# Later inverse deviations on GpSimd, first-norm transposes behind the next scores, and a new table of filler matmuls

## The chip, the cores and the metric

The kernel runs on one core of one Trainium2 chip. Its time is device microseconds for one execution. It was run three times: median 441.17 us, lowest 440.37, highest 441.78. One more execution was profiled; all rows below come from that one. Five engines work at once, each on its own queue of instructions, and meet through semaphores: TensorE (PE, with PEld for its weight loads), VectorE (DVE), ScalarE (ACT), GpSimd (POOL) and SyncE (SP, which only issues DMAs here).

## What is computed

A masked convolution with a row-by-row gated recurrence comes first (its scan runs over 16 rows). Its result, 16 images of 256 tokens with 96 channels, then goes through one transformer layer:

```python
x = _L0_conv_ref(x, w_i2s, w_s2s, w_skip, b_skip)
t = _to_tokens(x)
t = t + _L1_attn_ref(_ln_t(t), Wq, Wk, Wv, Wp, bp)      # causal, 6 heads of 16
t = t + _L1_ffn_ref(_ln_t(t), gate_w, gate_b, w1, b1, w2, b2)
x = _from_tokens(t, x)
...
def _ln_t(v, eps=1e-05):
    m = jnp.mean(v, axis=-1, keepdims=True)
    s = jnp.var(v, axis=-1, keepdims=True)
    return (v - m) / jnp.sqrt(s + eps)
...
# _L1_ffn_ref: 4 experts, the best 2 of a token kept and renormed
h = jax.nn.gelu(jnp.einsum('bsd,edh->ebsh', x, w1) + b1[:, None, None, :], approximate=False)
y = jnp.einsum('ebsh,ehd->ebsd', h, w2) + b2[:, None, None, :]
out = jnp.einsum('bse,ebsd->bsd', masked, y)
```

## The kernel before

The convolution and its recurrence take about the first 75 us. What follows is eight **passes** over blocks of two images: 512 tokens, as four **tiles** (s = 0 to 3) of 128 tokens. In the code a pass is `body(n, ...)`, once for each engine. Pass 0 is `first`, pass 7 is `last`, passes 1 to 6 are alike and follow one another at a fixed distance.

Attention inside a pass is cut into ten **units** u = 0 to 9 (`UNITS`): one tile's queries with three heads (tiles 0 and 2) or two heads (tiles 1 and 3). Units 0 and 1 are tile 0, units 2 to 4 tile 1, units 5 and 6 tile 2, units 7 to 9 tile 3. A unit goes through all engines:

- `scores(u)` on PE, into one of two PSUM banks;
- `row_max(u)` on DVE, `exps(u)` on ACT, `recip(u)` on DVE (one over the row sums);
- `scale(u)` on POOL, which multiplies the probabilities by those reciprocals;
- `probs_t(u)`, called T(u) here, on PE: transposes of the probabilities. It waits for `scale(u)`;
- `take_pt(u)`: a copy out of PSUM, on ACT for the units in `PT_ON_ACT`, on DVE for 0, 3, 5 and 7;
- `values(u)` on PE, and at a tile's end `heads_out(s)` (ACT), `project_out(s)` (PE) and `attn_residual(s)` (DVE), which adds the residual and takes mean and variance for the second norm.

The second norm then needs `rstd2(s)` on POOL (two small instructions, a sum and a power -0.5, called the pair here) and `normalize2(s)` on DVE. The expert layer of the pass stands at its end: transposes of the normed tokens, twelve hidden chunks, and routing.

The second expert matmul of pass n-1 is kept as **filler** for PE in pass n: 48 parts `expert_out(n-1, parts)`, 12 for each tile, each two matmul instructions; the first part of a tile has a bias matmul in front (the `b2hl` one). `FILL[j]` says how many parts stand in **slot** j, the piece of the pass's code with T(j) in it; what `FILL` leaves (12 parts, tile 3) is done behind the last slot. When a tile's 12 parts are done, DVE's `combine(s)` weighs its four experts' results: four instructions, put by line 831 into the slot after the one that holds the tile's last part. The first norm of pass n+1 runs in pass n's slots as well: `tokens_first` in slot 1, `norm1` and `rstd1` in slot 2, `normalize1` in slot 3, `channels_first` (four transposes of the normed tokens on PE) in slot 4, and `x1_rest` on DVE in slot 5.

Nothing is scheduled by a tool. Each engine's order is the order of the calls in its `body`, and an engine that waits holds up all that stands behind it in its own queue. The places that matter for the steps below:

- PE, lines 1090 to 1109: in slot j first `scores(j+2)`, then the filler, then `values`, then T(j), then `channels_first` (slot 4) and `project_out`.
- DVE, lines 821 to 843: in slot j `row_max(j+2)`, `recip(j+1)`, `take_pt(j)`, `x1_rest` (slot 5), `combine`, the norm steps, then `attn_residual` and `normalize2`.
- POOL, lines 452 to 459: in slot j `scale(j+1)`, then `rstd1` (slot 2), then `rstd2`.

Of the kernel before, what the change touches and what calls it, by code (L numbers as in the profile page):

```python
# [23 lines left out]
ALU = mybir.AluOpType  # L24
# [14 lines left out]
SPB = 4  # L39
# [12 lines left out]
NU = len(UNITS)  # L52
TILE_END = [1 + max(u for u, (a, t, _) in enumerate(UNITS) if 2 * a + t == s) for s in range(SPB)]

FILL = [16, 3, 3, 2, 3, 3, 2, 2, 2, 0]
TAIL = SPB * NCH - sum(FILL)
TAIL_EARLY = min(TAIL, 9)
PT_ON_ACT = (1, 2, 4, 6, 8, 9)
# [6 lines left out]
def hybrid_kernel(nc, x, w_input, w_state, b_skip, wq, wk, wv, wp, bp,  # L65
                  gate_w, gate_b, w1, b1, w2, b2, ident, ident_bf, causal_bf, lower, out):
    with ExitStack() as ctx:
# [331 lines left out]
        def _(pool):  # L399
# [9 lines left out]
            def rstd1(n):  # L409

                wait_alone(pool, ln1_aggr, 4 * n + 4)
                nc.gpsimd.tensor_scalar(ve1[:], mv1[:, :, 1], 1e-5, None, ALU.add).then_inc(rs1_step, 1)
                pool.wait_ge(rs1_step, 2 * n + 1)
                nc.gpsimd.tensor_tensor(rs1[:], ve1[:], nhalf[:], ALU.pow).then_inc(rs1_step, 1)

            def rstd2(n, s):
                wait_alone(pool, ln2_aggr, 4 * n + s + 1)
                nc.gpsimd.tensor_scalar(ve2[:, s:s + 1], mv2[:, s, 1:2], 1e-5, None, ALU.add).then_inc(rs2_step, 1)
                pool.wait_ge(rs2_step, 8 * n + 2 * s + 1)
                nc.gpsimd.tensor_tensor(rs2[:, s:s + 1], ve2[:, s:s + 1], nhalf[:, 0:1], ALU.pow).then_inc(rs2_step, 1)  # L420

# [28 lines left out]
            def body(n, first=False, last=False):  # L450
                scale(n, 0)
                for j in range(NU):
                    if j + 1 < NU:
                        scale(n, j + 1)
                    if j == EARLY_T0 + 1 and not last:
                        rstd1(n + 1)
                    for s in range(SPB - 1):
                        if j == TILE_END[s] + 1:
                            rstd2(n, s)
                rstd2(n, SPB - 1)  # L460
                keep_t1(n, first)
                if not last:
                    residual(n + 1)
                    x1_whole(n + 1)
# [157 lines left out]
        def _(dve):  # L622
# [131 lines left out]
            def normalize2(n, s):  # L754
                dve.wait_ge(rs2_step, 8 * n + 2 * s + 2)
                V.tensor_scalar(xh2[:, s], t1[:, s], mv2[:, s, 0:1], rs2[:, s:s + 1],
                                ALU.subtract, ALU.mult).then_inc(xh2_done, 1)
# [55 lines left out]
            def body(n, first=False, second=False, last=False):  # L813
# [7 lines left out]
                for j in range(NU):  # L821
# [17 lines left out]
                    for s in range(SPB - 1):  # L839
                        if j == TILE_END[s] + 1:  # L840
                            attn_residual(n, s, first)
                        if j == TILE_END[s] + 2:
                            normalize2(n, s)
                attn_residual(n, SPB - 1)
                if not last:
                    q_rest(n + 1)
# [32 lines left out]
        def _(pe):  # L879
# [207 lines left out]
            def body(n, first=False, last=False):  # L1087
                tail = [divmod(i, NCH) for i in range(SPB * NCH - TAIL, SPB * NCH)]
                for j in range(NU):
                    if j:  # L1090
                        if j + 2 < NU:
                            scores(n, j + 2)
                        if not first:
                            expert_out(n - 1, out_parts(j))
                        for u in VALUES_AT.get(j, ()):
                            values(n, u, first)
                    else:
                        start = [] if first else out_parts(0)
                        expert_out(n - 1, start[:NCH])
                        scores(n, 2)  # L1100
                        expert_out(n - 1, start[NCH:])
                    probs_t(n, j, first)
                    if j == EARLY_T0 and not last:
                        pe.wait_ge(v_done, n + 1)
                        tokens_first(n + 1)
                    if j == EARLY_XT and not last:
                        pe.wait_ge(t1_done, 4 * n + 1)
                        channels_first(n + 1)
                    for s in range(SPB - 1):
                        if j == TILE_END[s] + 1:  # L1110

# [145 lines left out]
```

## Time and profile before

| | |
|---|---|
| median of three runs | 441.17 us (440.37 to 441.78) |
| profiled execution | 441.85 us, of which the span from first to last instruction is 439.9 us |
| PE busy | 412.5 us, 94% of the span |
| DVE, ACT, POOL busy | 264.9, 252.1, 147.7 us |
| one pass of passes 1 to 6 | 42.17 us |
| granted TensorE clock | 0.987 on the mean; 1.00 in passes 1 to 7 |

A timeline row gives the start of a group in us from the span's start, the time from its first start to its last end, engine, line, operation, output and inputs, and a count. Ends of matmuls are modelled and overlap the next one, so the pace of PE is read from one start to the next. In brackets stands the idle time of the engine just before, and what ended it.

### The profile page before, as it was taken

The numbers are of one execution on the slowest core, as the hardware profiler recorded it, in microseconds if no ns is written. First come the engines' busy times: TensorE is split into PE (matmuls) and PEld (weight loads), VectorE is DVE, ScalarE is ACT, GpSimd is POOL, SyncE is SP. The second block draws the span as 40 slices with busy tenths as digits, with TensorE's granted clock in tenths as the row PEclk, the third lists the DMA queues.
The fourth block names the chain that finished last, engine by engine and source line by source line (L and its number), as shares of the span: only waits on it lengthen the run. The fifth ranks groups of instructions, "written<-read, shape, count | busy, mean of one in ns | idle before, by whom it ended". The sixth has DMA issues, their size and how long they took to land.

```text
span 439.9 us, 10654 instructions
## 1 busy us (share of the span) xinstructions
PE 412.5 (94%) x3226; PEld 346.7 (79%) x3226; DVE 264.9 (60%) x888; ACT 252.1 (57%) x701; POOL 147.7 (34%) x313
## 2 busy tenths in 40 slices
PE   4999999788899999999999999999999999999896
PEld 4999996455578878877887788788877887788686
DVE  2799998457416861785287538744863586267415
ACT  2333333356487648765865596568656764876380
POOL 6000000625513632462156305531543254236200
PEclk9999999969999999999999999999999999999999
DMA  8600000210021012101210120022002100210000
GB/s 185 168 0 0 0 0 19 63 30 17 9 60 44 3 34 53 39 1 42 52 31 0 48 55 22 0 55 52 18 0 61 46 0 7 77 24 4 7 14 18
DMA packets 16472, 14.94 MB, mean 34 GB/s; under 512 B 7586, under 2 KB 13588, under 8 KB 16452
## 3 DMA queue, kind: packets, MB, share of 16 engines
q1 hardware_dynamic: 14788, 13.87, 12.5%
q10 hardware_dynamic: 1472, 0.68, 0.6%
q8 instruction: 10, 0.16, 0.2%
q0 software_dynamic: 192, 0.15, 0.1%
q14 instruction: 10, 0.08, 0.1%
HBM read 3.86 MB, written 1.57 MB: 12 GB/s over the span
## 4 chain that ended last, share of the span: by engine, by line
PE 62%; DVE 16%; issue 10%; POOL 5%; ACT 2%; DVEq 1%; DMA 1%; ACTq 1%; POOLq 0%; SPq 0%
PE F L1057 13%; PE T L1015 6%; PE A L1036 6%; PE F L1073 4%; PE F L1077 4%; PE F L1074 4%; PE S L999 3%; POOL p_sb L435 3%; PE S L1001 3%; DVE fc L660 2%; DVE ig L659 2%; PE S L1004 2%; DVE t_cm L678 2%; DVE xh L713 1%; DVE nmax L735 1%
## 5 line engine op out<-in xcount | busy, mean ns | idle before, releaser
L435 POOL TENSOR_SCALAR p_sb<-p_sb,rden 128x128 f32<-128x128 f32 (+1 forms) x192 | 79.7, 431 | 121.1 <-DVE rden L741 119.0
L1057 PE MATMUL F<-w_sb,hid 128*128 128x96 f32 x768 | 97.6, 272 | 0.0
L1057 PEld LDWEIGHTS F<-w_sb,hid 128*128 128x128 f32 x768 | 95.6, 192 | 0.0
L551 ACT ACTIVATE p_sb<-S,nmax 128x128 f32<-128x128 f32 (+1 forms) x192 | 78.8, 424 | 12.7 <-DVE nmax L735 12.6
L735 DVE TENSOR_REDUCE nmax<-S 128x2 f32<-128x512 f32 (+1 forms) x80 | 50.5, 632 | 56.8 <-PE S L1004 56.7
L597 ACT ACTIVATE hid<-F,b_sb 128x512 f32<-128x512 f32 x72 | 49.5, 687 | 10.5 <-PE F L1077 9.7
L1015 PE MATMUL T<-id_sb,p_sb 128*128 128x128 f32 x288 | 48.5, 287 | 7.4 <-POOL p_sb L435 6.7
L484 ACT COPY pt_sb<-T 128x512 f32<-128x512 f32 (+1 forms) x48 | 26.4, 550 | 46.0 <-PE T L1015 46.0
L1015 PEld LDWEIGHTS T<-id_sb,p_sb 128*128 128x128 f32 x288 | 31.5, 145 | 17.6 <-POOL p_sb L435 12.2
L999 PE MATMUL S<-k_bd,q_st 96*128 96x384 f32 (+2 forms) x96 | 39.4, 417 | 3.5 <-DMA k_bd<-k_cur 2.7
L551 ACT ACTIVATION_READ_ACCUMULATOR p_sb<-S,nmax 128x1 f32 x192 | 39.7, 207 | 0.0
L1036 PE MATMUL A<-pt_sb,v_cur 128*32 128x128 f32 x576 | 33.9, 281 | 0.7 <-ACT pt_sb L484 0.7
L896 PE MATMUL F<-x_pad,win_sb 96*112 (+1 forms) x192 | 27.2, 291 | 6.2 <-DMA x_pad<-in_x 6.2
L1001 PE MATMUL S<-k_bd,q_st 96*128 96x384 f32 (+2 forms) x96 | 32.7, 348 | 0.0
L810 DVE SCALAR_TENSOR_TENSOR y_sb<-F,gw,y_sb 128x96 f32<-128x96 f32 x96 | 30.5, 317 | 3.4
L506 ACT ACTIVATE tc_sb<-cell 48x128 f32<-48x128 f32 x32 | 9.8, 307 | 37.7 <-DVE cell L662 37.7
L1073 PE MATMUL F<-x2hi,w1hi 96*128 96x512 f32 x72 | 29.9, 416 | 1.4 <-ACT x2hi L592 0.8
L896 PEld LDWEIGHTS F<-x_pad,win_sb 96*112 96x112 f32 x192 | 24.9, 193 | 6.1 <-DVE win_sb L632 6.1
L1077 PE MATMUL F<-x2lo,w1hi 96*128 96x512 f32 x72 | 29.2, 406 | 0.0
L1074 PE MATMUL F<-x2hi,w1lo 96*128 96x512 f32 x72 | 28.5, 395 | 0.0
L1036 PEld LDWEIGHTS A<-pt_sb,v_cur 128*32 128x32 f32 x576 | 21.5, 110 | 8.7 <-ACT pt_sb L484 5.5
L484 DVE COPY pt_sb<-T 128x384 f32<-128x384 f32 (+1 forms) x32 | 20.0, 624 | 13.0 <-PE T L1015 13.0
(142 smaller groups left out, 789.6 us busy)
## 6 DMA issues: line engine op xcount, KB each, us to landing
k_bd<-k_cur SPq DMA_DIRECT2D x93, 32.0 KB, 2.0
q_st<-q_cur SPq DMA_DIRECT2D x28, 96.0 KB, 2.2
k_bd<-k_cur SPq DMA_DIRECT2D x93, 16.0 KB, 1.8
t_st<-t_cm SPq DMA_DIRECT2D x7, 192.0 KB, 2.4
out_y<-y_sb SPq DMA_DIRECT2D x7, 192.0 KB, 1.9
x_pad<-in_x SPq DMA_DIRECT2D x2, 612.0 KB, 7.1
w_sb<-in_w SPq DMA_DIRECT2D x1, 576.0 KB
hid<-in_w SPq DMA_DIRECT2D x1, 576.0 KB, 6.9
```

What stands on the lines that cost most here:

```text
L435: last = nc.gpsimd.tensor_scalar(p, p, rden[:, u % 3, i:i + 1], 1.0, ALU.mult, ALU.mult)
L484: copy(pt_sb[:, u % NPT, 0:w], T[:, 0:w]).then_inc(pt_done, 1)
L551: last = nc.scalar.activation(p_sb[:, u % 3, i * nk:(i + 1) * nk], S[u % 2][:, i * nk:(i + 1) * nk], ACT.Exp, bias=nmax[:, u % 3, i:i + 1] ...
L597: nc.scalar.activation(hid[:, c, :], L1[c % 4][:], ACT.Gelu, bias=b1_sb[:, c:c + 1]).then_inc(gelu_done, 1)
L735: V.tensor_reduce(nmax[:, u % 3, 0:HG[t]], S[u % 2][:, 0:HG[t] * nk].rearrange("p (h k) -> p h k", k=nk), AX.X, ALU.max, negate=True).then ...
L896: last = mm(G[q][0:GATE_M, c * HC:(c + 1) * HC], wi_sb[:, tap, c], xr[:, bs, tap:tap + W], start=(c == 0 and tap == 0), stop=ready, skip_g ...
L999: mm(d, q_st[:, g, ts], k_bd[:, a, 0, g, i0:i1, 0:nk], start=(3 * g + i0 == h0), stop=False, skip_group_check=True)
L1015: last = nc.tensor.transpose(T[:, i * TT:(i + 1) * TT], p_sb[:, u % 3, i * TT:(i + 1) * TT], id_sb[:])
L1036: last = mm(A[VW * (h % 3):VW * (h % 3) + VW, 0:TT], v, pt_sb[:, u % NPT, c0:c0 + TT], start=(kt == 0 and h < 3), stop=(kt == t and h >= 3 ...
L1057: last = mm(dst[:, e * C:(e + 1) * C], hid[:, c, s * TT:(s + 1) * TT], w2_sb[:, c], start=False, stop=(c == NCH - 1), skip_group_check=True)
L1073: mm(dst, w1hi[:, cs], x2hi[:], start=True, stop=False)
L1077: mm(dst, w1hi[:, cs], x2lo[:], start=False, stop=True).then_inc(hid_ready, 1)
```

## The change

Four things, all in the order of work, and one in a POOL instruction's form:

- `rstd2(s)` on POOL moves one slot later for tiles 0 and 1: the pair of tile 0 stands behind `scale(5)` instead of `scale(4)`, that of tile 1 behind `scale(8)` instead of `scale(7)`. For tile 2 it stays behind `scale(9)`. `normalize2` on DVE moves one slot later with it.
- `channels_first(n+1)` on PE moves from the end of slot 4 to slot 5, behind `scores(7)`.
- `FILL` is new. The running sums of parts were 16, 19, 22, 24, 27, 30, 32, 34, 36, 36; they are 12, 15, 18, 20, 23, 27, 30, 33, 36, 36. The first slot's parts are split 8 and 4 around `scores(2)` instead of 12 and 4.
- From these sums follows more: the bias matmul of tile 1 goes from slot 0 to slot 1, that of tile 2 from slot 4 to slot 5; tile 1's last part (number 23) is in slot 5 instead of slot 3, so `combine(1)` on DVE goes from slot 4 to slot 6.
- The two `tensor_scalar` instructions that add 1e-5 on POOL now multiply by 1.0 and then add.

```diff
-FILL = [16, 3, 3, 2, 3, 3, 2, 2, 2, 0]
+FILL = [12, 3, 3, 2, 3, 4, 3, 3, 3, 0]
+FILL_AHEAD = 8
...
-                nc.gpsimd.tensor_scalar(ve1[:], mv1[:, :, 1], 1e-5, None, ALU.add).then_inc(rs1_step, 1)
+                nc.gpsimd.tensor_scalar(ve1[:], mv1[:, :, 1], 1.0, 1e-5, ALU.mult, ALU.add).then_inc(rs1_step, 1)
...
-                nc.gpsimd.tensor_scalar(ve2[:, s:s + 1], mv2[:, s, 1:2], 1e-5, None, ALU.add).then_inc(rs2_step, 1)
+                nc.gpsimd.tensor_scalar(ve2[:, s:s + 1], mv2[:, s, 1:2], 1.0, 1e-5, ALU.mult, ALU.add).then_inc(rs2_step, 1)
...
-                        if j == TILE_END[s] + 1:
+                        if j == min(TILE_END[s] + 2, NU - 1):
                             rstd2(n, s)
...
-                        if j == TILE_END[s] + 2:
+                        if j == TILE_END[s] + 3:
                             normalize2(n, s)
+                normalize2(n, SPB - 2)
                 attn_residual(n, SPB - 1)
...
                             scores(n, j + 2)
+                        if j == EARLY_XT + 1 and not last:
+                            pe.wait_ge(t1_done, 4 * n + 1)
+                            channels_first(n + 1)
                         if not first:
                             expert_out(n - 1, out_parts(j))
...
-                        expert_out(n - 1, start[:NCH])
+                        expert_out(n - 1, start[:FILL_AHEAD])
                         scores(n, 2)
-                        expert_out(n - 1, start[NCH:])
+                        expert_out(n - 1, start[FILL_AHEAD:])
                     probs_t(n, j, first)
...
-                    if j == EARLY_XT and not last:
-                        pe.wait_ge(t1_done, 4 * n + 1)
-                        channels_first(n + 1)
```

DVE's queue before, in pass 1, slots 4 to 6 (`row_max(6)` to `row_max(8)`, `recip(7)`, `attn_residual(1)`); L810 is `combine(1)`, L756 `normalize2(0)`, L484 `take_pt(5)`, L718 `x1_rest`:

```order
L735 TENSOR_REDUCE nmax<-S 128x3
L741 RECIPROCAL rden<-den 128x3
L810 SCALAR_TENSOR_TENSOR y_sb<-F,gw,t1p 128x96
L810 SCALAR_TENSOR_TENSOR y_sb<-F,gw,y_sb 128x96 x3
L756 TENSOR_SCALAR xh<-t,mv,rs 128x96
L735 TENSOR_REDUCE nmax<-S 128x2
L741 RECIPROCAL rden<-den 128x3
L484 COPY pt_sb<-T 128x384
L718 TENSOR_TENSOR x1lo<-M,x1hi 96x512
L735 TENSOR_REDUCE nmax<-S 128x2
L741 RECIPROCAL rden<-den 128x2
L748 TENSOR_TENSOR t<-M,tb 128x96
```

The same place in the changed kernel (its lines are one higher):

```order
L736 TENSOR_REDUCE nmax<-S 128x3
L742 RECIPROCAL rden<-den 128x3
L736 TENSOR_REDUCE nmax<-S 128x2
L742 RECIPROCAL rden<-den 128x3
L485 COPY pt_sb<-T 128x384
L719 TENSOR_TENSOR x1lo<-M,x1hi 96x512
L757 TENSOR_SCALAR xh<-t,mv,rs 128x96
L736 TENSOR_REDUCE nmax<-S 128x2
L742 RECIPROCAL rden<-den 128x2
L811 SCALAR_TENSOR_TENSOR y_sb<-F,gw,t1p 128x96
L811 SCALAR_TENSOR_TENSOR y_sb<-F,gw,y_sb 128x96 x3
L749 TENSOR_TENSOR t<-M,tb 128x96
```

`combine(1)` stood ahead of `take_pt(5)`; it now stands behind `recip(7)`, ahead of `attn_residual(1)`, `row_max(9)` and `recip(8)`. `normalize2(0)` went from in front of `row_max(7)` to behind `x1_rest`.

POOL's queue before, in pass 0, from `scale(4)` to the pair of tile 2 (L435 is `scale`, three instructions for a unit of three heads and two for one of two heads; L418 and L420 are a pair):

```order
L435 TENSOR_SCALAR p_sb<-p_sb,rden 128x256 x2
L418 TENSOR_SCALAR ve<-mv 128x1
L420 TENSOR_TENSOR rs<-ve,nhalf 128x1
L435 TENSOR_SCALAR p_sb<-p_sb,rden 128x128 x6
L435 TENSOR_SCALAR p_sb<-p_sb,rden 128x256 x2
L418 TENSOR_SCALAR ve<-mv 128x1
L420 TENSOR_TENSOR rs<-ve,nhalf 128x1
L435 TENSOR_SCALAR p_sb<-p_sb,rden 128x256 x4
```

And in the changed kernel:

```order
L436 TENSOR_SCALAR p_sb<-p_sb,rden 128x256 x2
L436 TENSOR_SCALAR p_sb<-p_sb,rden 128x128 x3
L419 TENSOR_SCALAR ve<-mv 128x1
L421 TENSOR_TENSOR rs<-ve,nhalf 128x1
L436 TENSOR_SCALAR p_sb<-p_sb,rden 128x128 x3
L436 TENSOR_SCALAR p_sb<-p_sb,rden 128x256 x4
L419 TENSOR_SCALAR ve<-mv 128x1
L421 TENSOR_TENSOR rs<-ve,nhalf 128x1
L436 TENSOR_SCALAR p_sb<-p_sb,rden 128x256 x2
```

Tile 0's pair went from in front of `scale(5)` to in front of `scale(6)`, tile 1's from in front of `scale(8)` to in front of `scale(9)`.

## Rows read from the trace of the kernel before

**Rows 1.** The page, busy time, share and instructions of each engine.
```profile
PE 412.5 (94%) x3226; PEld 346.7 (79%) x3226; DVE 264.9 (60%) x888; ACT 252.1 (57%) x701; POOL 147.7 (34%) x313
```

**Rows 2.** Stretches: us, busy of PE, PEld, DVE, ACT, POOL, clock, DMA; pass 4.
```profile
259.90:302.07 42.17, 41.15 (x326) 34.14 (x326) 25.35 (x86) 28.07 (x80) 17.12 (x37) 1.00 0.13 33
```

**Rows 3.** Timeline of PE in pass 4.
```profile
263.40 0.42 PE L1053 MATMUL F<-b2hl,ones 128*128 128x384 f32 x1
263.67 1.02 PE L1057 MATMUL F<-w_sb,hid 128*128 128x96 f32 x8
264.53 0.49 PE L1015 MATMUL T<-id_sb,p_sb 128*128 128x128 f32 x3
...
272.38 0.62 PE L1015 MATMUL T<-id_sb,p_sb 128*128 128x128 f32 x4
273.12 0.65 PE L965 MATMUL M<-id_sb,xh 128*96 128x128 f32 x4
273.57 0.49 PE L999 MATMUL S<-k_bd,q_st 96*128 96x512 f32 x1
...
276.02 0.55 PE L1015 MATMUL T<-id_sb,p_sb 128*128 128x128 f32 x3
...
280.40 0.58 PE L1057 MATMUL F<-w_sb,hid 128*128 128x96 f32 x4
281.59 0.66 PE L1015 MATMUL T<-id_sb,p_sb 128*128 128x128 f32 x4 [0.61 <-POOL p_sb L435]
...
283.49 0.66 PE L1015 MATMUL T<-id_sb,p_sb 128*128 128x128 f32 x4
```

**Rows 4.** Timeline of POOL in pass 4.
```profile
262.69 1.08 POOL L435 TENSOR_SCALAR p_sb<-p_sb,rden 128x128 f32<-128x128 f32 x3 [9.91 <-DVE rden L741]
...
271.35 0.94 POOL L435 TENSOR_SCALAR p_sb<-p_sb,rden 128x256 f32<-128x256 f32 x2
...
274.70 1.10 POOL L435 TENSOR_SCALAR p_sb<-p_sb,rden 128x128 f32<-128x128 f32 x3
...
278.60 0.94 POOL L435 TENSOR_SCALAR p_sb<-p_sb,rden 128x256 f32<-128x256 f32 x2 [1.04 <-DVE rden L741]
279.62 0.23 POOL L418 TENSOR_SCALAR ve<-mv 128x1 f32<-128x1 f32 x1
...
280.60 0.94 POOL L435 TENSOR_SCALAR p_sb<-p_sb,rden 128x256 f32<-128x256 f32 x2
281.83 0.94 POOL L435 TENSOR_SCALAR p_sb<-p_sb,rden 128x256 f32<-128x256 f32 x2 [0.29 <-DVE rden L741]
```

**Rows 5.** Timeline of DVE in pass 4.
```profile
274.05 0.29 DVE L810 SCALAR_TENSOR_TENSOR y_sb<-F,gw,t1p 128x96 f32<-128x96 f32 x1
...
275.32 0.33 DVE L756 TENSOR_SCALAR xh<-t,mv,rs 128x96 f32<-128x96 f32 x1
275.56 0.68 DVE L735 TENSOR_REDUCE nmax<-S 128x2 f32<-128x512 f32 x1
...
276.61 0.56 DVE L484 COPY pt_sb<-T 128x384 f32<-128x384 f32 x1 [0.28 <-PE T L1015]
...
278.28 0.15 DVE L741 RECIPROCAL rden<-den 128x2 f32<-128x2 f32 x1
...
279.77 0.16 DVE L741 RECIPROCAL rden<-den 128x2 f32<-128x2 f32 x1
...
282.48 0.26 DVE L748 TENSOR_TENSOR t<-M,tb 128x96 f32<-128x96 f32 x1 [0.82 <-PE M L1042]
...
283.32 0.32 DVE L810 SCALAR_TENSOR_TENSOR y_sb<-F,gw,t1p 128x96 f32<-128x96 f32 x1
```

**Rows 6.** Stretches in pass 0, columns as in Rows 2.
```profile
86.58:89.27 2.69, 0.00 (x0) 0.03 (x1) 2.69 (x3) 2.47 (x2) 1.11 (x2) 1.00 0.52 138
90.00:100.40 10.40, 9.54 (x44) 6.34 (x42) 5.44 (x18) 5.74 (x24) 3.79 (x10) 0.51 0.15 38
...
111.43:112.80 1.37, 0.00 (x1) 0.01 (x1) 1.00 (x3) 0.54 (x3) 1.27 (x4) 1.00 0.02 6
```

## What I expected of the change

> **What bounds the kernel now.** I read four views, in this order. The page's first table says PE is busy 94% of the span and no other engine more than 60% [rows 1], so the first guess is that only PE's own work counts. That share is no proof, since matmul records overlap. The stretch of one pass comes next: passes 1 to 6 each take 42.17 us, at the full granted clock [rows 2], so one pass can be worked through and multiplied. The third view is PE's timeline of such a pass, read from start to start. It shows where PE stands. At T(4), the transposes start at 272.38 and `channels_first` at 273.12, 0.74 later, though four transposes take 0.45 (273.12 to 273.57): about 0.3 is lost to a wait for the normed tokens. At T(8) PE is through its filler by about 280.98 and starts at 281.59, 0.61 later, for POOL's `scale(8)` [rows 3]. These two are what the change is aimed at. The fourth view is the two queues behind T(8). POOL ends `scale(7)` at 279.54, does the pair of tile 1 from 279.62, and only then `scale(8)` at 280.60 [rows 4]. But DVE's `recip(8)` ended at 279.77 + 0.16 = 279.93 [rows 5], so with the pair gone `scale(8)` could start no more than 0.50 sooner: from a reciprocal's end to the scale takes 0.17 (278.28 + 0.15 to 278.60 [rows 4, 5]). **So DVE's queue stands right behind POOL's**, and what the change does to DVE decides. That queue is in order: in slot 8 the last filler is done near 281, so `combine(2)` has its input, DVE then idles 0.82 before 282.48 for a projection, and `combine(2)` still starts at 283.32, after that projection's norm [rows 3, 5].
>
> **The change, part by part.** All shifts are against the same point of pass 4.
>
> *Slot 0, four parts less.* They are 8 matmuls, 263.67 to 264.53, 0.86 us, and the bias of tile 1, 263.40 to 263.67, 0.27 [rows 3]. PE would reach T(0) 1.13 sooner, at 263.40. But T(0) waits for `scale(0)`, which ends at 262.69 + 1.08 = 263.77 [rows 4] and hangs on steps that don't move (exps of unit 0 behind the table load, routing on DVE). T(0) starts at 263.82: 0.71 won, 0.42 turned into a wait. That cover gone, splitting the filler 8 and 4 buys nothing more: `scores(2)` comes sooner, yet T(0) is last. In slot 1 the bias returns (0.27) and I allow 0.1 for PE to fill again behind the stop (0 to 0.2; no row shows it alone). At T(1) 0.33 is left. Slots 1 to 3 hold the same three, three and two parts, so ACT, DVE and POOL all move by the same 0.33.
>
> *Slot 4, the bias of tile 2 gone.* PE comes 0.27 sooner still, but T(4) waits for `scale(4)`, 271.35 + 0.94 = 272.29 [rows 4], less 0.33. T(4) starts at 272.01, 0.37 sooner, and I give its four transposes 0.45 plus 0.05 of the same allowance.
>
> *`channels_first` behind `scores(7)`.* `scores(7)` starts at 272.51, since its bank is free. The wait of 0.3 goes: the tokens are ready long before their new place. `x1_rest` needs them only behind `take_pt(5)`, so the later place costs nothing.
>
> *Slot 5, one part more and the bias.* Before, from `scores(7)` to T(5) was 276.02 - 273.57 = 2.45 [rows 3]. Now 0.45 (`channels_first`), 0.21 (a part is two matmuls of 0.86/8) and 0.27 come in: 3.38. **T(5) starts at 272.51 + 3.38 = 275.89, only 0.13 sooner**, although three parts (0.64) and a wait of 0.3 were taken out ahead of it. The difference is the new waits at T(0) and T(4) and the restarts. It could be as early as `scale(5)` lets it: that is now straight behind `recip(5)`, which ends near 274.1 (the combine next to it starts at 274.05) and moves by 0.3, so 0.17 and 1.10 later it is 275.1 [rows 4, 5]: 0.88 sooner. The other end is 0.2 later.
>
> *`combine(1)` and `normalize2(0)` on DVE.* Behind T(5), `take_pt(5)` starts 0.59 later (276.02 to 276.61 [rows 3, 5]): 276.48. From there to the end of `recip(8)` DVE worked without a stop for 279.93 - 276.61 = 3.32. Into that stretch now come `combine(1)`, 274.05 to 275.32, 1.27, and `normalize2(0)`, 275.32 to 275.56, 0.24 [rows 5]. Both stood earlier, where DVE now has nothing to do: it will idle for over 1 us ahead of `take_pt(5)`, which waits for T(5), with both queued behind. `recip(8)` ends at 276.48 + 3.32 + 1.51 = 281.31, 1.38 later. Behind it on other engines wait `scale(8)` and so T(8); `exps(9)` waits for the `row_max(9)` just ahead.
>
> *The pair of tile 1 behind `scale(8)`.* `scale(8)` starts 0.17 behind `recip(8)`, at 281.48, ends 0.94 later at 282.42, and T(8) starts at 282.47 (0.05 later, as 281.54 to 281.59 before [rows 3, 4]). That is **0.88 later than before**: -0.13 + 1.51 - 0.50. PE has three more parts in slots 6 to 8 to fill the wait, and still stands there for more than 1 us.
>
> *The pair ahead of `scale(9)`.* It starts 0.08 behind `scale(8)` and holds POOL for 0.98 (279.62 to 280.60). `scale(9)` runs from 283.48 to 284.42, T(9) starts at 284.47 instead of 283.49 [rows 3, 4]: 0.98 later. The way through PE from T(8) to T(9) took 1.90, so it would be at 284.37; POOL is last by 0.1.
>
> *Costed at nothing.* `normalize2(1)` now waits on DVE for the pair, with `attn_residual(2)` behind it, some 0.3; PE's last values, q and k projections lie between T(9) and the next projection and cover it, and without that cover it would cost 0.3. The pair of tile 0 ahead of `scale(6)` ends in time for T(6), which has one part more in front. The two-op form: the trace has only one-op adds of 0.23 and two-op scales of 0.36 for 128 columns (1.08 for three) [rows 4]; I take 0, between -0.1 and +0.1, with at most two of five in a pass on the path. No DMA and no queue of SP is touched. Behind T(9) all of a pass hangs together and moves as one.
>
> **Sum.** 0.98 in each of passes 1 to 7 (pass 7 has the same filler and combine in the same slots) is 6.9. Pass 0 has no filler and no combine: there the pair leaves the way to T(8) and comes back in front of T(9), I take -0.2, between -0.9 (nearly the whole 0.98) and +0.3 (the pair of tile 0 now holding up `scale(6)`). Together +6.7 on the profiled execution's 441.85, of which 439.9 is span; it ran 0.68 above the median of 441.17, and I add to the median: **447.9 us**. With T(5) and the restarts within some 0.25 of my reading, a pass loses 0.6 to 1.2, and the time is 444.5 to 449.9.
>
> **Rivals.**
>
> 1. *PE arrives early.* If the new waits at T(0) and T(4) don't show, T(5) starts 0.88 sooner, T(8) is 0.13 and T(9) 0.23 late: 7 x 0.23 - 0.2 = +1.4, 442.6. For it: nearly 1 us of PE work is taken out ahead. Against: the end of `scale(0)` at 263.77. It decides from T(5) about 1 us sooner on: there the sign turns.
> 2. *DVE is not last, so the kernel gets faster.* If `combine(1)` ran beside DVE's waits after all, T(8) would be set by PE, whose four matmuls from 280.40 need 0.43: 280.83, 0.13 sooner, with 0.64 more filler, is 281.34 rather than 281.59 [rows 3]. 7 x -0.25 - 0.2 = -2.0, 439.2. It decides as soon as the idle time before `take_pt(5)` is used for the 1.27. For it: that idle time is as long as the combine. Against: the order of the queue, and 283.32, which shows it kept.
> 3. *The clock falls.* PE stood 2.69 us before 89.27; from 90.00 to 100.40 the granted clock was 0.51, the 1.2 GHz level. It stood 1.37 before 112.80 and kept 1.00, 2.4 GHz [rows 6]. The new stop at T(8) is near the second. If it acted like the first, ten slow microseconds in each of seven passes cost up to 5 each, +35: 483. The Trainium skill, "TensorE: Matmul & The Clock Gate", section "What's actually happening", has the half clock as the default that only activity lifts; by that rule a longer stop is dangerous, and the row of 2.69 agrees, while the row of 1.37 says this one is short enough.
> 4. *Nothing comes of it:* the moves cancel, 441.2.
>
> **How the numbers follow.** My forecast 0.68, rival 1 0.12, rival 2 0.13, rival 3 0.02, rival 4 0.05. A difference under 0.3% (1.3 us) can't be told from none. Rival 1 lies on that border and is split in halves. Slower: 0.68 + 0.02 + 0.06 = 0.76; same: 0.06 + 0.05 = 0.11; faster: 0.13. The range goes from 442.0, to take in rival 1, to 450.2, for the forecast's upper end; it leaves out rivals 2 to 4, which is 0.20.
>
> **What would show it.** In the changed profile: a pass of about 43.1; PE waiting for POOL's `p_sb` at T(0) and T(4), and over 1 us at T(8); DVE idle for over 1 us ahead of `take_pt(5)` and then without a stop to `recip(8)`; `scale(8)` 0.17 behind `recip(8)` with the pair after it; no wait ahead of `channels_first`. I am wrong if T(5) comes more than 0.5 sooner within the pass, if DVE still has idle time between `take_pt(5)` and `recip(8)`, or if a pass is below 42.2.

## The result, and the profile after

The changed kernel took 443.63 us (median of 11 runs, 441.39 to 444.58), the kernel before 441.27 beside it (11 runs, 440.37 to 443.00): a ratio of 1.004, with a 95% interval of 1.0024 to 1.0057. By the medians it is slower by 2.4 us, 0.5%. The forecast was 447.9, slower by 6.7. The direction and the place were right; the size was nearly three times too large. The time lies inside the range of 442.0 to 450.2 only because that had been widened to take in rival 1; it is below the 444.5 to 449.9 of the forecast itself.

The profiled execution of the changed kernel took 443.63 us, its span is 441.7. First the page's line of busy times, then one stretch with the columns of [rows 2]: pass 4 from the same point as there.

```profile
PE 413.0 (93%) x3226; PEld 347.9 (79%) x3226; DVE 266.2 (60%) x888; ACT 252.8 (57%) x701; POOL 144.3 (33%) x313
```

```profile
260.17:302.70 42.53, 41.20 (x326) 34.27 (x326) 25.47 (x86) 28.20 (x80) 16.72 (x37) 1.00 0.13 32
```

A pass takes 42.53 instead of 42.17, at the full clock as before: 0.36 more, where 0.98 was forecast. The busy times don't show it; only the stretch does. PE's timeline of that pass, which answers to [rows 3] (L1017 is T, L967 `channels_first`, L1055 the bias, L1059 filler, L1142 the transposes of the second norm's tokens, called x2T here, once a pass):

```profile
246.96 0.64 PE L1142 MATMUL T<-id_sb,xh 128*96 128x128 f32 x4
...
263.09 1.03 PE L1059 MATMUL F<-w_sb,hid 128*128 128x96 f32 x8
264.08 0.55 PE L1017 MATMUL T<-id_sb,p_sb 128*128 128x128 f32 x3
...
271.42 0.80 PE L1059 MATMUL F<-w_sb,hid 128*128 128x96 f32 x6
272.11 0.65 PE L1017 MATMUL T<-id_sb,p_sb 128*128 128x128 f32 x4
272.52 0.47 PE L1001 MATMUL S<-k_bd,q_st 96*128 96x512 f32 x1
...
273.18 0.60 PE L967 MATMUL M<-id_sb,xh 128*96 128x128 f32 x4
273.62 0.36 PE L1059 MATMUL F<-w_sb,hid 128*128 128x96 f32 x2
273.76 0.42 PE L1055 MATMUL F<-b2hl,ones 128*128 128x384 f32 x1
...
275.78 0.55 PE L1017 MATMUL T<-id_sb,p_sb 128*128 128x128 f32 x3
...
282.29 0.66 PE L1017 MATMUL T<-id_sb,p_sb 128*128 128x128 f32 x4 [1.12 <-POOL p_sb L436]
...
284.18 0.66 PE L1017 MATMUL T<-id_sb,p_sb 128*128 128x128 f32 x4
...
289.49 0.64 PE L1142 MATMUL T<-id_sb,xh 128*96 128x128 f32 x4
```

In the kernel before x2T of pass 3 starts at 246.69; all shifts below are measured from this point. The wait at T(8) is 1.12, where 0.61 stood in [rows 3]. POOL's timeline, which answers to [rows 4] (L436 is `scale`, L419 and L421 a pair):

```profile
262.95 1.07 POOL L436 TENSOR_SCALAR p_sb<-p_sb,rden 128x128 f32<-128x128 f32 x3 [9.90 <-DVE rden L742]
...
271.10 0.95 POOL L436 TENSOR_SCALAR p_sb<-p_sb,rden 128x256 f32<-128x256 f32 x2
274.07 1.06 POOL L436 TENSOR_SCALAR p_sb<-p_sb,rden 128x128 f32<-128x128 f32 x3 [2.02 <-DVE rden L742]
...
281.30 0.93 POOL L436 TENSOR_SCALAR p_sb<-p_sb,rden 128x256 f32<-128x256 f32 x2 [1.77 <-DVE rden L742]
282.31 0.19 POOL L419 TENSOR_SCALAR ve<-mv 128x1 f32<-128x1 f32 x1
282.59 0.55 POOL L421 TENSOR_TENSOR rs<-ve,nhalf 128x1 f32<-128x1 f32 x1
283.12 0.93 POOL L436 TENSOR_SCALAR p_sb<-p_sb,rden 128x256 f32<-128x256 f32 x2
```

And DVE's, which answers to [rows 5] (L742 is `recip`, L485 `take_pt`, L811 `combine`, L757 `normalize2`):

```profile
275.05 0.18 DVE L742 RECIPROCAL rden<-den 128x3 f32<-128x3 f32 x1 [0.56 <-ACT p_sb L552]
276.36 0.56 DVE L485 COPY pt_sb<-T 128x384 f32<-128x384 f32 x1 [1.14 <-PE T L1017]
...
278.35 0.29 DVE L811 SCALAR_TENSOR_TENSOR y_sb<-F,gw,t1p 128x96 f32<-128x96 f32 x1
278.68 1.02 DVE L811 SCALAR_TENSOR_TENSOR y_sb<-F,gw,y_sb 128x96 f32<-128x96 f32 x3
...
280.98 0.16 DVE L742 RECIPROCAL rden<-den 128x2 f32<-128x2 f32 x1
...
289.10 0.33 DVE L757 TENSOR_SCALAR xh<-t,mv,rs 128x96 f32<-128x96 f32 x1 [0.45 <-POOL rs L421]
```

The main steps read as forecast. DVE stands idle for 1.14 ahead of `take_pt(5)` with `combine(1)` queued behind it, then works without a stop until `recip(8)` ends at 281.14; `scale(8)` follows 0.16 later, and T(8) after that. What differs is how early the stretch begins and how long a pair takes. The new waits at T(0) and T(4) are hardly there: each starts 0.06 behind the end of its scale on POOL (264.02 and 272.05), as forecast, but PE is there at nearly the same time. From the eight filler matmuls to T(0) it is 0.99, where eight took 0.86 before, and from the six to T(4) 0.69, where six took 0.64; the profile marks neither as a wait.

### The profile page after: what moved, and what is told of

The parts are those of the page before. It is cut to its first block, busy times and chain, and to the rows that moved or that the text cites. A ratio compares the mean times of both kernels' runs of the same rounds, so it can differ in the third digit from the quotient of the medians.

```text
span 441.7 us, 10654 instructions
## 1 busy us (share of the span) xinstructions
PE 413.0 (93%) x3226; PEld 347.9 (79%) x3226; DVE 266.2 (60%) x888; ACT 252.8 (57%) x701; POOL 144.3 (33%) x313
## 4 chain that ended last, share of the span: by engine, by line
PE 64%; DVE 18%; issue 9%; POOL 3%; ACT 2%; DVEq 1%; DMA 1%; ACTq 1%; SPq 0%; POOLq 0%
PE F L1059 13%; PE T L1017 7%; PE A L1038 6%; PE F L1075 4%; PE F L1079 4%; PE F L1076 4%; PE S L1001 4%; PE S L1003 3%; PE S L1006 2%; DVE fc L661 2%; DVE ig L660 2%; DVE y_sb L811 2%; POOL p_sb L436 2%; DVE t_cm L679 2%; DVE nmax L736 1%
## 5 line engine op out<-in xcount | busy, mean ns | idle before, releaser
L436 POOL TENSOR_SCALAR p_sb<-p_sb,rden 128x128 f32<-128x128 f32 (+1 forms) x192 | 79.0, 426 | 140.5 <-DVE rden L742 140.0
L1059 PE MATMUL F<-w_sb,hid 128*128 128x96 f32 x768 | 98.6, 271 | 0.0
L1059 PEld LDWEIGHTS F<-w_sb,hid 128*128 128x128 f32 x768 | 96.5, 192 | 0.0
L1017 PE MATMUL T<-id_sb,p_sb 128*128 128x128 f32 x288 | 49.3, 290 | 10.1 <-POOL p_sb L436 9.8
L485 ACT COPY pt_sb<-T 128x512 f32<-128x512 f32 (+1 forms) x48 | 26.4, 550 | 42.6 <-PE T L1017 42.6
L1017 PEld LDWEIGHTS T<-id_sb,p_sb 128*128 128x128 f32 x288 | 31.1, 144 | 20.5 <-POOL p_sb L436 14.4
L811 DVE SCALAR_TENSOR_TENSOR y_sb<-F,gw,y_sb 128x96 f32<-128x96 f32 x96 | 30.5, 318 | 3.4
L485 DVE COPY pt_sb<-T 128x384 f32<-128x384 f32 (+1 forms) x32 | 19.8, 619 | 10.4 <-PE T L1017 10.0
```

The lines of the kernel that those rows point to most:

```text
L436: last = nc.gpsimd.tensor_scalar(p, p, rden[:, u % 3, i:i + 1], 1.0, ALU.mult, ALU.mult)
L485: copy(pt_sb[:, u % NPT, 0:w], T[:, 0:w]).then_inc(pt_done, 1)
L1017: last = nc.tensor.transpose(T[:, i * TT:(i + 1) * TT], p_sb[:, u % 3, i * TT:(i + 1) * TT], id_sb[:])
L1059: last = mm(dst[:, e * C:(e + 1) * C], hid[:, c, s * TT:(s + 1) * TT], w2_sb[:, c], start=False, stop=(c == NCH - 1), skip_group_check=True)
```

## The experiments

Theory A is the prediction's: the new table puts `combine(1)`, 1.27 us, into the stretch from `take_pt(5)` to `recip(8)`, and T(8) hangs on that. Rival R: the table costs on PE itself, through new waits at T(0) and T(4) and later filler. Rival P: the pair of tile 1 ahead of `scale(9)` costs. Each kernel was timed in five rounds beside the kernel before, on one chip for all of a group. The pass is read from x2T of pass 3 to x2T of pass 4 in its trace. It is the sharper measure: it is free of pass 0, where the clock makes one run 2 to 3 us longer than the next (last section).

| kernel | us | before beside it | ratio, 95% interval | pass |
|---|---|---|---|---|
| before | 441.27 | | | 42.17 |
| the change | 443.63 | 441.27 | 1.004 (1.0024 to 1.0057) | 42.53 |
| table alone | 447.90 | 441.79 | 1.0138 (1.0102 to 1.0174) | 43.15 |
| pairs alone | 439.72 | 441.79 | 0.9947 (0.9926 to 0.9968) | 41.98 |
| transposes alone | 441.02 | 441.53 | 0.9993 (0.9974 to 1.0011) | 41.97 |
| form alone | 438.38 | 440.66 | 0.9943 (0.9918 to 0.9968) | 41.87 |
| change, old table | 437.05 | 441.79 | 0.9899 (0.9859 to 0.9939) | 41.60 |
| change, `combine(1)` in slot 8 | 437.40 | 441.79 | 0.9893 (0.9855 to 0.9930) | 41.64 |
| change, `combine(1)` early | 438.52 | 441.53 | 0.9931 (0.9908 to 0.9954) | 41.75 |
| change, old form | 445.68 | 441.53 | 1.0106 (1.0083 to 1.0128) | 42.87 |

**Is it the table, and is it `combine(1)`?** Three kernels decide that.

The table alone, on the kernel before:

```diff
-FILL = [16, 3, 3, 2, 3, 3, 2, 2, 2, 0]
+FILL = [12, 3, 3, 2, 3, 4, 3, 3, 3, 0]
+FILL_AHEAD = 8
...
-                        expert_out(n - 1, start[:NCH])
+                        expert_out(n - 1, start[:FILL_AHEAD])
```

> The kernel before with the new table of fillers and the 8 and 4 split alone; pairs, transposes of the first norm and the one-operation form as before. Theory A: combine(1) goes into slot 6 while the pair of tile 1 still stands ahead of scale(8), but recip(8) is now so late that the pair is done before it; T(8) and T(9) late by 0.5 to 0.9 us a pass, the time 445 to 448, slower than the whole change (443.6). Rival P: the pairs are where they were, so no loss: 439 to 442. Rival R: slower too, 443 to 446.

It is the slowest of all, 0.98 a pass. T(8) comes 0.99 late. So the other three parts of the change win, and the table loses more than they win. Rival P falls as the cause: with the pairs at their old places the loss is larger, not smaller.

The change with the old table:

```diff
-FILL = [12, 3, 3, 2, 3, 4, 3, 3, 3, 0]
-FILL_AHEAD = 8
+FILL = [16, 3, 3, 2, 3, 3, 2, 2, 2, 0]
+FILL_AHEAD = NCH
```

> The changed kernel with the old table of fillers (16, 3, 3, 2, 3, 3, 2, 2, 2, 0, the first slot split 12 and 4); the later inverse deviations, the later transposes of the first norm and the two-operation form stay. Theory A (the loss comes from combine(1), 1.27 us, having gone into the stretch from take_pt(5) to recip(8) on which scale(8) and T(8) hang): combine(1) is back in slot 4, where DVE is idle, and what is left of the change helps. T(8) should be about 0.1 to 0.5 us earlier in a pass than in the kernel before, the pass 41.6 to 41.9, the time 436 to 439. Rival P (the pair of tile 1 ahead of scale(9) is what costs): the pair is still there, so the time stays near 443. Rival R (the table costs on PE itself) expects a faster kernel here too; it is told apart by the combine runs.

4.7 us faster than the kernel before, as A expected. Now the one that parts A from R, the changed kernel with its new table, and only `combine(1)` elsewhere:

```diff
                         for s, c in out_parts(j - 1):
-                            if c == NCH - 1:
+                            if c == NCH - 1 and s != 1:
                                 combine(n - 1, s, second)
+                        if j == 8:
+                            combine(n - 1, 1, second)
```

> The changed kernel, its new table and all, with only combine(1) moved two slots later on DVE, behind recip(9) and take_pt(8)'s place in slot 8. Theory A: the stretch from take_pt(5) to recip(8) is 1.27 us shorter, scale(8) ends before PE reaches T(8), so T(8) is 0.4 to 1.2 us earlier than in the changed kernel, the pass 41.5 to 41.9, the time 435 to 439. Rival R (the table costs on PE, through the waits at T(0) and T(4) and the filler's later place, whatever DVE does): stays at 443 to 444. Rival P (the pair ahead of scale(9)): stays at 443 to 444 as well, with T(9) waiting for scale(9).

437.40, a pass 0.89 shorter than the change's. PE's order is the changed kernel's word for word, and T(0) and T(4) stand where they stood (17.13 and 25.18 behind x2T of pass 3, 17.12 and 25.15 in the changed kernel). R falls, and A stands. DVE's timeline of this kernel, from `take_pt(5)` over `recip(8)` (277.08) to `combine(1)` in its new place:

```profile
273.75 0.56 DVE L485 COPY pt_sb<-T 128x384 f32<-128x384 f32 x1 [1.14 <-PE T L1019]
...
277.08 0.16 DVE L742 RECIPROCAL rden<-den 128x2 f32<-128x2 f32 x1
277.94 0.69 DVE L485 COPY pt_sb<-T 128x512 f32<-128x512 f32 x1 [0.71 <-PE T L1019]
278.66 0.17 DVE L742 RECIPROCAL rden<-den 128x2 f32<-128x2 f32 x1
278.83 0.32 DVE L811 SCALAR_TENSOR_TENSOR y_sb<-F,gw,t1p 128x96 f32<-128x96 f32 x1
```

From `take_pt(5)` to the start of `recip(8)` it is 3.33 here and 4.62 in the changed kernel (276.36 to 280.98): 1.29 less, about the length of `combine(1)`. The 1.14 of idle time ahead of `take_pt(5)` is the same in both; it was never the loss, only room that went unused. A fourth kernel uses it:

```diff
-FILL = [12, 3, 3, 2, 3, 4, 3, 3, 3, 0]
+FILL = [12, 3, 3, 2, 4, 3, 3, 3, 3, 0]
...
+                    if not first and j == 5:
+                        combine(n - 1, 1, second)
                     if j not in PT_ON_ACT:
                         take_pt(dve, n, j, first)
...
-                    if not first and j:
+                    if not first and j and j != 5:
```

> The changed kernel with one part of filler moved from slot 5 to slot 4 (so that tile 1 is done there) and combine(1) put in slot 5 ahead of take_pt(5), into the idle time that DVE has there (0.56 and 1.14 us). Theory A: combine(1) costs 1.27 and finds 1.2 to 1.7 of idle time if its last part comes in time; the stretch from take_pt(5) to recip(8) is 1.27 shorter, T(8) is set by PE: pass 41.6 to 42.0, the time 436.5 to 440. Rival R (the table costs on PE whatever DVE does): 443 to 444. A third case: the part comes too late, take_pt(5) is pushed back by up to 0.8 and half the gain goes: 440 to 442.

DVE's timeline of it, from `recip(6)` to `take_pt(5)`:

```profile
272.61 0.17 DVE L742 RECIPROCAL rden<-den 128x3 f32<-128x3 f32 x1 [0.56 <-ACT p_sb L552]
272.78 0.32 DVE L811 SCALAR_TENSOR_TENSOR y_sb<-F,gw,t1p 128x96 f32<-128x96 f32 x1
273.13 1.02 DVE L811 SCALAR_TENSOR_TENSOR y_sb<-F,gw,y_sb 128x96 f32<-128x96 f32 x3
274.07 0.55 DVE L485 COPY pt_sb<-T 128x384 f32<-128x384 f32 x1
```

`combine(1)` stands in the idle time, `take_pt(5)` follows without a gap, 0.82 behind T(5) (273.25) instead of 0.58. A pass is 0.78 shorter than the change's. The same work on the same engine costs 0.89 us a pass in the stretch behind `take_pt(5)`, and 0.11 ahead of it, each against its place behind `recip(9)` (the early place also has one part of filler moved).

**What are the other three parts worth?** Each alone, on the kernel before. The pairs:

```diff
-                        if j == TILE_END[s] + 1:
+                        if j == min(TILE_END[s] + 2, NU - 1):
                             rstd2(n, s)
...
-                        if j == TILE_END[s] + 2:
+                        if j == TILE_END[s] + 3:
                             normalize2(n, s)
+                normalize2(n, SPB - 2)
```

> The kernel before with only the inverse deviations of tiles 0 and 1 and their normalize2 one slot later; old table, old place of the first norm's transposes, one-operation form. Theory A: scale(8) starts up to 0.50 us sooner, T(8) up to 0.5 sooner, limited by PE to about 0.13 to 0.3; the pair comes back ahead of scale(9) and takes part of it: 0 to -0.3 us a pass, pass 0 -0.8, the time 438 to 441. Rival P: the pair (0.98) ahead of scale(9) makes T(9) late by 0.3 or more in each pass: 442 to 445, slower than before.

0.19 a pass. T(8) is 0.17 sooner and T(9) 0.19. More could not come at T(8): PE now waits there for `take_pt(7)`, the copy out of the PSUM tile that T(8) writes, and T(8) starts 1.53 behind T(7), where it was 1.69 (279.90 to 281.59). So of the 0.50 that the prediction gave as the most, about 0.16 was to be had at this place; it had not looked at that copy. The pair does come back ahead of `scale(9)`: that ends at 281.69 and T(9) starts at 281.75. But this is 1.88 behind T(8), and PE's own way there takes 1.86 to 1.90 in the other kernels where POOL is done in time. Rival P's mechanism is in reach, and costs some hundredths at most. POOL's timeline of this kernel, the pair of tile 1 and `scale(9)`:

```profile
279.73 0.23 POOL L418 TENSOR_SCALAR ve<-mv 128x1 f32<-128x1 f32 x1
280.04 0.57 POOL L420 TENSOR_TENSOR rs<-ve,nhalf 128x1 f32<-128x1 f32 x1
280.70 0.99 POOL L435 TENSOR_SCALAR p_sb<-p_sb,rden 128x256 f32<-128x256 f32 x2
```

The first norm's transposes:

```diff
                             scores(n, j + 2)
+                        if j == EARLY_XT + 1 and not last:
+                            pe.wait_ge(t1_done, 4 * n + 1)
+                            channels_first(n + 1)
...
-                    if j == EARLY_XT and not last:
-                        pe.wait_ge(t1_done, 4 * n + 1)
-                        channels_first(n + 1)
```

> The kernel before with only the transposes of the first norm moved from the end of slot 4 to slot 5, behind scores(7). Theory A with the prediction's own price: the wait of 0.3 us ahead of them goes and nothing else, T(5) 0.24 to 0.3 sooner than before. If the prediction's price was too small (the experiments with the old and the new table so far suggest that the move alone is worth more), T(5) is 0.4 to 0.5 sooner. Behind T(5) the pair of tile 1 still holds up scale(8), so T(8) gains less than T(5): about 0.2 to 0.4, and the time 438.5 to 440.5. If the move is worth nothing, 441.8 as before.

The medians can't tell it from no change; the passes can, 41.97 against 42.17. The time is above the range that was expected. T(5) is only 0.17 sooner, less than either price, because PE then stands ahead of it for `scale(5)`: 273.45 + 1.09 = 274.54, T(5) at 274.60. The pair of tile 0 stands ahead of that scale. With the pair moved too (the change with the old table, which has the new form as well) T(5) is 0.40 sooner. Here the parts need one another. POOL's timeline of the kernel with the transposes alone, the pair of tile 0 and `scale(5)`:

```profile
272.48 0.23 POOL L418 TENSOR_SCALAR ve<-mv 128x1 f32<-128x1 f32 x1 [1.45 <-DVE mv L752]
272.79 0.57 POOL L420 TENSOR_TENSOR rs<-ve,nhalf 128x1 f32<-128x1 f32 x1
273.45 1.09 POOL L435 TENSOR_SCALAR p_sb<-p_sb,rden 128x128 f32<-128x128 f32 x3
```

The form of the two additions, taken back in the changed kernel, and the other way round put alone into the kernel before:

```diff
-                nc.gpsimd.tensor_scalar(ve1[:], mv1[:, :, 1], 1.0, 1e-5, ALU.mult, ALU.add).then_inc(rs1_step, 1)
+                nc.gpsimd.tensor_scalar(ve1[:], mv1[:, :, 1], 1e-5, None, ALU.add).then_inc(rs1_step, 1)
...
-                nc.gpsimd.tensor_scalar(ve2[:, s:s + 1], mv2[:, s, 1:2], 1.0, 1e-5, ALU.mult, ALU.add).then_inc(rs2_step, 1)
+                nc.gpsimd.tensor_scalar(ve2[:, s:s + 1], mv2[:, s, 1:2], 1e-5, None, ALU.add).then_inc(rs2_step, 1)
```

> The changed kernel with the two additions of 1e-5 on POOL in their old form with one operation. If the new form is cheaper as the two traces read (a pair 0.81 instead of 0.98 us from its start to the start of the scale behind it), scale(9) ends 0.17 later than in the changed kernel, 0.05 after PE would reach T(9): T(9) 0.1 later, the rest of the pass with it, and normalize2(1) 0.17 later: the time 444.0 to 445.0. If the form costs the same (what the prediction took) and the shorter pair has another cause, nothing changes: 443.6.

> The kernel before with only the form of POOL's two additions changed to two operations; the order of all work is as before. The changed kernel with the old form lost 0.34 us a pass against the changed kernel, so: if the form is worth that wherever a pair stands ahead of a scale that is last (here scale(4) behind the first norm's pair, scale(8) behind the pair of tile 1), T(8) is 0.2 to 0.3 sooner, a pass 41.8 to 42.0, the time 439.0 to 440.5. If the form is worth nothing, as the prediction took it, 441.5 as before.

This part, which the prediction put at nothing, is the largest of the three: 0.30 a pass alone, and without it the change loses 0.70 a pass instead of 0.36. The 445.68 is above the 444.0 to 445.0 that was expected, which had counted `scale(9)` and tile 1's `normalize2` and not the other pairs. POOL's timeline with the old form in the changed kernel, at the place of the rows 281.30 to 283.12 above:

```profile
280.74 0.94 POOL L436 TENSOR_SCALAR p_sb<-p_sb,rden 128x256 f32<-128x256 f32 x2 [1.77 <-DVE rden L742]
281.76 0.23 POOL L419 TENSOR_SCALAR ve<-mv 128x1 f32<-128x1 f32 x1
282.07 0.57 POOL L421 TENSOR_TENSOR rs<-ve,nhalf 128x1 f32<-128x1 f32 x1
282.74 0.99 POOL L436 TENSOR_SCALAR p_sb<-p_sb,rden 128x256 f32<-128x256 f32 x2
```

From the pair's start to the scale behind it is 0.98, as in [rows 4], and 0.81 in the new form. With 0.98, `scale(9)` ends at 283.73 and T(9) waits for it (283.79); with 0.81 it ends at 284.05, 0.13 ahead of T(9).

The account of a pass, each part alone: +0.98 - 0.19 - 0.20 - 0.30 = +0.29. Together they measure +0.36. That the two are so close is in part chance. Alone, each of the three smaller parts ends up with T(8) 1.53 behind T(7), so they win at one and the same place and can't simply be added: without the table they win 0.57 together (42.17 to 41.60), not 0.69.

**Is there a version that is faster than both?** The change with the old table is one. What holds it then? At T(8) PE waits 0.46, no longer for POOL: the PSUM tile that T writes is still being read by `take_pt(7)`. T(8) in PE's timeline of that kernel:

```profile
277.94 0.63 PE L1017 MATMUL T<-id_sb,p_sb 128*128 128x128 f32 x4 [0.46 <-DVE pt_sb L485]
```

I read a second wait at T(6), for `scale(6)` behind the pair of tile 0, and tried to fill it (before: `[16, 3, 3, 2, 3, 3, 2, 2, 2, 0]`):

```diff
+FILL = [16, 3, 3, 2, 3, 3, 3, 2, 1, 0]
```

> The kernel with the old table and the rest of the change (437.05), with one part of filler moved from slot 8 to slot 6. There PE waits about 0.26 us at T(6) for scale(6), which the pair of tile 0 now holds up. Theory: the part (0.21) fills that wait, T(8) comes 0.2 sooner with scale(8) still ahead of it, the pass goes from 41.60 to about 41.40, the time to 435.5. Rival: T(6) is not waiting as read, or scale(9), 0.37 ahead of T(9), becomes last: unchanged at 437.

436.80 (ratio 0.9909, 0.9876 to 0.9943), a pass 41.63: nothing. The wait at T(6) was filled, and the one at T(8) grew to 0.68: from T(7) over `take_pt(7)` to T(8) it is 1.53 whatever PE has to do between. Filling T(8)'s wait instead:

```diff
+FILL = [15, 3, 3, 3, 2, 3, 2, 2, 3, 0]
```

> The kernel with the old table and the rest of the change (41.60 us a pass), with one part of filler taken from slot 0 and one more in slot 8 (15, 3, 3, 3, 2, 3, 2, 2, 3, 0); combine(1) stays in slot 4 and all other queues are as they were. PE waits 0.46 at T(8) for take_pt(7), and T(0) has 0.77 in hand ahead of scale(0)'s end. Theory: all from T(0) to T(8) comes 0.14 to 0.21 sooner and the part fills the wait at T(8): a pass 41.4 to 41.46, the time 1.0 to 1.4 below the old-table kernel, 435.6 to 436.1. Rival: scale(4) or scale(6), with 0.17 and 0.05 in hand, don't come sooner with PE, and nothing is won: 437.

```diff
+FILL = [14, 3, 3, 4, 2, 2, 2, 2, 4, 0]
```

> As the kernel before it, with two parts taken from slot 0 and two more in slot 8 (14, 3, 3, 4, 2, 2, 2, 2, 4, 0). Theory: 0.28 to 0.42 a pass if scale(1) and scale(6) follow PE: 41.2 to 41.3, the time 434.2 to 435.2. Rival: the wait moves to T(1) and T(4), as it did at T(0) and T(4) in the changed kernel, and the second part wins nothing more than the first: 435.6 to 436.1 or 437.

436.40 (0.9900, 0.9866 to 0.9934) and 435.92 (0.9895, 0.9859 to 0.9932), passes 41.63 and 41.54: both came as their rivals said. PE does come sooner, to T(5) by 0.27 and 0.35, and gives it back at T(6), all of it or all but 0.05, as PE's timeline of the kernel with 15 shows:

```profile
273.15 0.55 PE L1017 MATMUL T<-id_sb,p_sb 128*128 128x128 f32 x3 [0.41 <-POOL p_sb L436]
```

`scale(6)` does not move with PE. In the old-table kernel two things release it at the same moment: the pair of tile 0 on POOL (272.47 + 0.55, the scale starts at 273.01), and `recip(6)` on DVE, which stands behind `combine(1)` (272.66 + 0.17, and 0.17 more is 273.00). POOL's and DVE's timelines of the old-table kernel there:

```profile
272.47 0.55 POOL L421 TENSOR_TENSOR rs<-ve,nhalf 128x1 f32<-128x1 f32 x1
273.01 1.06 POOL L436 TENSOR_SCALAR p_sb<-p_sb,rden 128x128 f32<-128x128 f32 x3
```

```profile
272.66 0.17 DVE L742 RECIPROCAL rden<-den 128x3 f32<-128x3 f32 x1
```

By these rows, to take one of them away would win nothing; no run took only one. Both away, on the table with 15:

```diff
-                        if j == min(TILE_END[s] + 2, NU - 1):
+                        if j == min(TILE_END[s] + (2 if s else 3), NU - 1):
                             rstd2(n, s)
...
-                            if c == NCH - 1:
+                            if c == NCH - 1 and s != 1:
                                 combine(n - 1, s, second)
+                        if j == 8:
+                            combine(n - 1, 1, second)
...
-                        if j == TILE_END[s] + 3:
+                        if j == TILE_END[s] + (3 if s else 4):
                             normalize2(n, s)
```

> The kernel with one part moved from slot 0 to slot 8 (15, 3, 3, 3, 2, 3, 2, 2, 3, 0; 41.63 us a pass, where PE waits 0.41 at T(6) for scale(6)). Two things that stand ahead of scale(6) are moved behind it: the pair of tile 0 one slot later again on POOL (behind scale(6), its normalize2 in slot 6), and combine(1) on DVE from slot 4 to slot 8, so that recip(6) comes sooner. Theory: scale(6) is held by both at once (the pair's end and recip(6) lie together in the old-table kernel); with both away it ends 0.4 or more sooner, T(6) is set by PE, T(8) follows until take_pt(7) is last: a pass 41.2 to 41.4, the time 434 to 435.5. Rival: DVE's later work (combine(1) ahead of combine(2) and normalize2(1)) delays attn_residual(2) and the end of the pass, or the chain from T(7) over take_pt(7) to T(8) keeps all: 436 to 437.

433.77 us beside 440.74, a ratio of 0.9843 (0.9814 to 0.9872), a pass 41.22: 1.6% faster than the kernel before and the best of the study. T(6) comes without a wait, and at T(8) 0.23 is left, again for `take_pt(7)`. PE's timeline of it, T(6) to T(8):

```profile
272.00 0.49 PE L1019 MATMUL T<-id_sb,p_sb 128*128 128x128 f32 x3
...
274.45 0.66 PE L1019 MATMUL T<-id_sb,p_sb 128*128 128x128 f32 x4
...
275.98 0.63 PE L1019 MATMUL T<-id_sb,p_sb 128*128 128x128 f32 x4 [0.23 <-DVE pt_sb L485]
```

## Why the prediction was right in kind and wrong in size

The shifts in pass 4, in us; with the old form the kernel is the one that the forecast had in mind, since it took the form as free:

| | forecast | the change | the change, old form |
|---|---|---|---|
| T(0) | -0.71 | -0.72 | -0.70 |
| T(4) | -0.37 | -0.54 | -0.43 |
| T(5) | -0.13 | -0.51 | -0.39 |
| T(8) | +0.88 | +0.43 | +0.56 |
| T(9) | +0.98 | +0.42 | +0.71 |
| a pass | +0.98 | +0.36 | +0.70 |

So the mechanism held, and two terms of the sum were mis-sized. They make up nearly all of the 0.62 between the forecast and the measured loss of a pass.

- **T(0)** was right to 0.01: bound by `scale(0)`, 0.7 won out of 1.13. The stop there was not the 0.42 that the forecast gave it, but 0.13; some 0.2 more went in front of `scores(2)` (16 filler matmuls and the step to it took 1.91, 24 of them 2.59 before).
- **`combine(1)` and `normalize2(0)`**, the term that decides, was right: from `take_pt(5)` to `recip(8)`'s end 4.78 (276.36 to 281.14), forecast 4.83. No wait ahead of `channels_first` and the 1.14 of idle time came as forecast too.
- **T(5) was mis-sized**, by 0.26 of the 0.62 (old form). The allowances for PE starting again behind a stop, 0.1 in slot 1 and 0.05 at T(4), were not there. T(4), which follows T(1) through `scale(4)`, was 0.06 sooner than forecast. From T(4) to `scores(7)` it was 0.41, not 0.50, and from there to T(5) 3.27 with the old form and 3.26 with the new, not 3.38: a part of filler took 0.14 (273.62 to 273.76), not the 0.21 that 0.86/8 gives, and each of the other pieces some hundredths less. In the changed kernel T(5) is 0.51 sooner, and "more than 0.5 sooner" was the prediction's own sign of being wrong: it came, just. Rival 1 decides from T(5) 1 us sooner on; at 0.5 it went about half the way, and its 442.6 lies nearer to the measured time than the forecast does.
- **The two-operation form was mis-sized**, by 0.34 of the 0.62. The step took 0 with bounds of 0.1 either way "with at most two of five in a pass on the path". Three of the five pairs count: the first norm's, from its start to `scale(4)` 1.37 instead of 1.47 (T(4) to T(8) 0.11 to 0.13 sooner); tile 1's, 0.81 instead of 0.98 to `scale(9)` (T(9) no longer set by POOL, another 0.16); and tile 3's, 0.05 at x2T, which starts 5.31 behind T(9) instead of 5.36. That last wait is in the trace of before, and the prediction had not looked at it: PE's timeline of the kernel before at x2T of pass 3.

```profile
246.69 0.64 PE L1140 MATMUL T<-id_sb,xh 128*96 128x128 f32 x4 [0.15 <-DVE xh L756]
```

In the changed kernel no wait is marked at that row (246.96 above); with the old form it is 0.16 again. The order is the same in all three: x2T starts 0.38 to 0.39 behind the start of tile 3's `normalize2` (289.10 to 289.49 above), so what the prediction called moving as one behind T(9) still hangs on this pair.

- **Pass 0** moved by -0.77 (x2T from 120.22 to 119.45), forecast -0.2 with bounds of -0.9 and +0.3. T(8) of pass 0 went from 112.80 to 112.09: the pair is out of its way and costs nothing on its return, since T(9) follows 1.90 later as before (1.89). It was the lower bound that was near. It takes another 0.57 off the forecast.
- **The sum**: 6 times 0.36, 0.48 in pass 7 and -0.77 give +1.9, close to the 1.8 by which the spans differ (439.9 to 441.7; the medians differ by 2.4), for a forecast of +6.7.
- **The other rivals**: rival 2 (DVE is not last) did not come about in the changed kernel, but its mechanism is what the early and the late `combine(1)` do; their 438.5 and 437.4 lie below the 439.2 worked out for it. Rival 3 (the clock falls) did not either: PE stood 1.1 at T(8) in each of passes 1 to 6 and 0.49 in pass 7, and the granted clock of passes 1 to 7 is 1.00. Rival 4 (the moves cancel) is shut out by the interval.

## What to carry to other kernels

Where an engine works strictly in the order of its code, the place of a piece of work matters more than its amount: 1.27 us of DVE work cost 0.9 us a pass behind a wait that many things hang on, and 0.1 ahead of that wait, both against a place behind the stretch. A table that moves PE's filler moves other engines' work with it; before changing it, ask which engine's steps are keyed to it and where they land. And when a wait is taken away and nothing is won, look whether the next thing that the instruction waits for ends at almost the same time.

## What the runs showed of the hardware

**A POOL instruction's bar doesn't hold what it costs the next one on POOL.** By the bars, the new form saves 0.04 us on the addition (0.23 to 0.19) and 0.02 on the power (0.57 to 0.55). By the starts, the pair and its gaps go from 0.98 to 0.81, and most of that lies between the start of the power and the start of the scale behind it: 0.67 (282.07 to 282.74) against 0.53 (282.59 to 283.12). The Trainium skill, "Perfetto Trace Analysis", section "GPSIMD Engine Instruction", advises to time such instructions by the spacing of their starts and not by the reported duration; the traces agree, 0.17 by the starts and 0.06 by the bars. For another engine that waits for the pair the bars come near: tile 3's `normalize2` on DVE starts 0.85 behind the start of the pair with the new form (288.25 to 289.10) and 0.91 with the old one (287.56 to 288.47 in the kernel before). Why the form with two operations is the shorter one, no run here shows.

**The half-clock stretch in pass 0 varies from run to run.** In the kernel before PE ran at the 1.2 GHz level for nearly all of 90.00 to 100.40 [rows 6], and so it did in the changed kernel. In other profiled executions, whose code up to there differs at most in the form of POOL's addition, the stretch was shorter. The same stretch with the columns of [rows 2], of the changed kernel and of the changed kernel with the old form:

```profile
90.00:100.40 10.40, 9.67 (x45) 6.47 (x43) 5.45 (x19) 5.73 (x24) 3.88 (x10) 0.52 0.15 38
```

```profile
90.00:100.40 10.40, 9.06 (x56) 5.88 (x54) 6.66 (x22) 7.72 (x34) 5.07 (x12) 0.88 0.14 36
```

In both PE had just stood still, for 2.90 and 2.94 us. With a granted clock of 0.88 instead of 0.52, x2T of pass 0 starts at 117.80 instead of 119.45, in a kernel whose later passes are 0.34 longer. The spread of the runs goes with it: those of the changed kernel with a mean clock of 0.996 took 441.4 to 441.8, the others 443.1 to 444.6. A difference of under 3 us between two single runs of this kernel says nothing; the length of a pass does.
